# Graph attention in one launch: a group of heads leaves PSUM one slot later, and a finished graph is summed behind the attention

## The reference, cut to what matters

```
mask = adjacency + eye > 0                       # first network
for l in range(3):
    scores = si[:, :, None] + sj[:, None, :] + attn_b[l]
    scores = where(scores >= 0, scores, 0.2 * scores); masked with -inf
    h = layernorm(x + softmax(scores) @ x, g1[l], beta1[l])
    x = layernorm(h + gelu(h @ W1[l] + b1[l]) @ W2[l] + b2[l], g2[l], beta2[l])
x = layernorm(x_in + x)
xp = x @ W_proj                                  # second network, 8 heads of 32
scores[b, h, i, j] = a_src[b, h, i] + a_dst[b, h, j] + b_att[h]
out = relu(softmax(masked leaky_relu(scores)) @ xh)
result = layernorm(x + out)
```

## Time and profile before

| | us |
|---|---|
| median of 3 runs (lowest, highest) | 2346.33 (2344.75, 2347.79) |
| the profiled execution, its own time | 2346.35 |
| span of the profile, first to last instruction | 2344.6 |
| busy: PE, PE weight load | 2217.9 (95%), 1564.2 (67%) |
| busy: DVE, ACT, POOL | 1806.8 (77%), 1686.4 (72%), 184.9 (8%) |
| DMA | 29.4% of the 16 engines' span |

### The profile page before, as it was taken

One profiled execution on the slowest core, in us unless ns is written; L12 is line 12 of the kernel. 1 busy time (PEld: TensorE's weight loads), 2 busy tenths in 40 slices (PEclk: granted clock), 3 DMA queues, 4 the chain that ended last, 5 costly groups with the idle time before them and its releaser, 6 DMA issues.

```text
span 2344.6 us, 32312 instructions
## 1 busy us (share of the span) xinstructions
PE 2217.9 (95%) x10497; PEld 1564.2 (67%) x10497; DVE 1806.8 (77%) x5718; ACT 1686.4 (72%) x3247; POOL 184.9 (8%) x200
## 2 busy tenths in 40 slices
PE   3999999999999999999999999999999999999765
PEld 2676767666776777667676677667767666767543
DVE  5457687878788788887788787887888877676577
ACT  2434468777877778777787778777688777878685
POOL 0010110000100010000100001000100000010000
PEclk9999999999999999999999999999999999999977
DMA  6011024343072242442253331622434421200011
GB/s 217 10 36 54 10 95 147 96 131 118 28 220 86 73 139 78 153 120 75 99 162 95 126 121 29 216 86 72 140 94 137 133 72 53 73 23 19 28 46 37
DMA packets 116019, 219.57 MB, mean 94 GB/s; under 512 B 7784, under 2 KB 57228, under 8 KB 110476
## 3 DMA queue, kind: packets, MB, share of 16 engines
q1 hardware_dynamic: 115852, 217.50, 29.4%
HBM read 164.78 MB, written 52.69 MB: 93 GB/s over the span
## 4 chain that ended last, share of the span: by engine, by line
PE 75%; DVE 16%; ACT 5%; issue 2%; POOL 1%; DMA 1%; SPq 0%; DVEq 0%; POOLq 0%; ACTq 0%
PE ffn L1198 22%; PE av L1115 13%; PE ffn L1187 11%; PE av L1187 11%; PE pT L1098 8%; PE av L1139 4%; DVE prob L751 2%; PE av L1174 2%; DVE prob L742 2%; ACT prob L505 2%; ACT prob L499 1%; DVE stats L690 1%; DVE xs L868 1%; DVE xs L862 1%; PE trow L1077 1%
## 5 line engine op out<-in xcount | busy, mean ns | idle before, releaser
L1198 PE MATMUL ffn<-w_sb,G 128*128 128x256 f32 x3072 | 743.7, 382 | 0.0
L1198 PEld LDWEIGHTS ffn<-w_sb,G 128*128 128x128 f32 x3072 | 562.5, 191 | 90.7 <-issue 24.3
L751 DVE CUSTOM_DVE_ANT_0 prob<-trow,mask 128x512 f32<-128x512 f32 x704 | 458.1, 685 | 56.3 <-PE trow L1077 32.6
L1098 PEld LDWEIGHTS pT<-ident,prob 128*128 128x128 f32 x2144 | 273.1, 146 | 185.4 <-issue 115.5
L1098 PE MATMUL pT<-ident,prob 128*128 128x128 f32 x2144 | 337.1, 283 | 49.1 <-DVE prob L805 18.8
L505 ACT ACTIVATE prob<-prob,nm 128x512 f32<-128x512 f32 x512 | 363.0, 712 | 0.0
L499 ACT ACTIVATE prob<-prob,s 128x512 f32<-128x512 f32 x512 | 349.3, 715 | 13.7 <-DVE nm L758 13.0
L1187 PE MATMUL ffn<-hT,w_sb 128*128 128x512 f32 x768 | 355.0, 595 | 1.1 <-ACT hT L518 1.1
L1187 PE MATMUL av<-hT,w_sb 128*128 128x512 f32 x768 | 353.6, 593 | 0.0
L455 POOL TENSOR_TENSOR rstd<-veps,mhalf 128x4 f32<-128x4 f32 x127 | 160.0, 1260 | 2115.2 <-DVE veps L686 2115.2
L1115 PE MATMUL av<-xs,prob 128*128 128x257 f32 x1024 | 244.3, 380 | 11.1 <-DVE prob L812 11.1
(11 more groups left out here) (120 smaller groups left out, 2579.1 us busy)
## 6 DMA issues: line engine op xcount, KB each, us to landing
w_sb<-in_L_gnn_W SPq DMA_DIRECT2D x48, 1024.0 KB, 8.4
blocks_dram<-blocks SPq DMA_DIRECT2D x168, 256.0 KB, 4.2
prob<-blocks_dram SPq DMA_DIRECT2D x42, 1024.0 KB, 4.8
trow<-rows_dram SPq DMA_DIRECT2D x128, 256.0 KB, 3.3
adj_sb<-in_adj SPq DMA_DIRECT2D x16, 1024.0 KB, 7.4
xin<-in_x SPq DMA_DIRECT2D x16, 512.0 KB, 6.3
x0r<-in_x SPq DMA_DIRECT2D x16, 512.0 KB, 5.8
out<-o SPq DMA_DIRECT2D x15, 512.0 KB, 4.0
```

The lines of the kernel that those rows point to most:

```text
L751: return v.tensor_tensor_reduce(out=out_[:, t, :], in0=targets, in1=mask[:, t, :], scale=1.0, scalar=LEAST, op0=ALU.add, op1=ALU.max, accu ...
L1098: last = te.transpose(pT[bank][:, j * P:(j + 1) * P], src[:, t, j * P:(j + 1) * P], ident[:])
L1198: last = te.matmul(ffn[part][:, at:at + D], G[:, f, t * P:(t + 1) * P], w2_sb[:, g // 2 % STAGES, f, :], start=f == 0, stop=f == FT - 1)
```

## The change

`heads_out` for four heads is no longer called at the end of the unit in which PE made them, but in the next unit, between `times_gain` and `first_targets`. `graph_sum` of an even graph (slot 4) is called behind `attention` and `turn_blocks` rather than before them; that of an odd graph (slot 1) stays. `graph_out` and `plus_bias` change places. POOL's inverse deviation of an even finished graph follows that of the attention. No instruction is added or taken away.

```diff
@@ gpsimd
-                if ended(g) is not None:
+                if ended(g) is not None and ended(g) % 2:
                     inverse_deviation(LAST)
                 if first_ends(g) is not None and g + 1 < UNITS:
                     inverse_deviation(RESIDUAL)
                 if g + 1 < UNITS:
                     inverse_deviation(ATTENDED)
+                if ended(g) is not None and ended(g) % 2 == 0:
+                    inverse_deviation(LAST)
@@ vector
-                four = side_by_side(turned(g))[1]
+
+                four = side_by_side(turned(g - 1))[1] if g else None
...
                 times_gain(s, l)
+                if four is not None:
+                    heads_out(four)
                 if att:
                     first_targets(s2)
...
                 done = ended(g)
-                if done is not None:
+                if done is not None and done % 2:
                     graph_sum(done)
...
                 for q in turned_behind(g)[:1]:
                     turn_blocks(q)
+                if done is not None and done % 2 == 0:
+                    graph_sum(done)
+                plus_bias(s, l)
                 if done is not None:
                     graph_out()
-                plus_bias(s, l)
                 if att:
                     fed_forward(s, 0)
...
                 for q in new[2:]:
                     head_made(q)
-                if four is not None:
-                    heads_out(four)
```

## The result

The changed kernel takes 2340.24 us (median of 9 runs, 2338.00 to 2340.75) where the kernel before took 2347.08 (9 runs, 2344.75 to 2350.72): 6.8 us less, a ratio of 0.997 with a 95% interval of 0.996 to 0.998. The forecast was 12.3 us less, 2334.1, with a range up to 2338.0. The sign was right, the size nearly twice too large, and the median lies outside the range. The span of the profile fell from 2344.6 to 2338.5 us.

The account below looks back on a forecast made before the run. PE, busy 2217.9 us, was taken to bound the kernel, so only its waits for DVE could give time. Five units at 2.00 plus 2.27 make 12.3 us, and 2346.35 less that gives 2334.1, range 2328.5 to 2338.

Parts of the forecast that it names:

- Part 1: Slot 4: with `graph_sum` of even graphs behind the attention, PE's wait before the third product goes, 12.3 us in all.
- the 2.00 that were forecast: Slot 4: PE's third product starts 4.35 us behind the first instead of 6.35, a gain in each of five units.
- The gain in unit 46: Slot 4 of the last pair: DVE itself waits 0.67 us for PE and PE isn't waiting, so nothing is gained.
- Part 2: `heads_out` a slot later, 0.89 us on DVE, moved 27 times: no cost or gain in slots 5, 1, 3 and 4.
- PE's 0.84 us: Slot 4: PE's delay at L1077 for DVE's row sums moves to the first product, awaiting ACT's probabilities; gain 0.
- the 3.31 us of `graph_sum`: Slot 4: DVE time of its four kinds of instruction, from L937 to L800, moved behind the attention and held covered.
- the 7.85 us: Slot 4: DVE's idle time before L898, until PE's L1147, taken as cover for the moved work.
- The rival "nothing": Slot 4: PE loses the 2.00 us again later, behind `normalise` for instance, and 2346 stays; chance 0.04.
- The rival "less": Slots 1, 3, 5: `heads_out` uncovered, first targets late, 0.34 us in each of 20 slots, 6.8 us; 2340.9; chance 0.08.

Follow-up runs that it names:

- e1: The kernel before with only `heads_out` moved a slot later: 2347.70 us against 2346.68 for the kernel before, ratio 1.0005.
- e4: The changed kernel with `heads_out` of slot 4 put behind `first_targets`: 2335.08 us against 2346.68 for the kernel before.
- e3: The changed kernel with DVE waiting for GpSimd's shift ahead of `graph_sum`: 2334.91 us against 2346.68 for the kernel before.
- e6: The changed kernel with slot 4's `heads_out` split, reciprocal ahead of the targets, product between attention and `graph_sum`: 2332.88 us against 2347.48 for the kernel before.
- e7: The changed kernel with `graph_sum`'s first instruction cut into four of 128x256: 2336.70 us against 2347.48 for the kernel before.

## Why the prediction was wrong

**Part 1, the wait before the third product: right.** It is gone in all six units. In unit 16 the third product comes 1.88 us sooner behind the first, the fourth another 0.07 sooner, and the first 0.06 sooner in the unit: the 2.00 that were forecast. The gain in unit 46 was nothing, as said: it takes 47.05 us in both traces.

**Part 2, `heads_out`: right.** It was priced at nothing in four places, and e1 shows no price that can be told from none. That PE's 0.84 us would move to the first product and hang on ACT was right as well (e4).

**The step that failed** is the one that priced what was moved behind the attention. The prediction counted the 3.31 us of `graph_sum` against the 7.85 us in which DVE is idle, found them covered, and said that what DVE, POOL and ACT do behind the last `attended` "is counted from PE's fourth product and comes earlier with it". It asked whether DVE has time for the moved work, not whom the work disturbs while it runs. GpSimd's L460 is 0.2 us long and on the chain from the attention to the next state (L455, L460, L541, L1174). Of POOL the text said only that it is 8% busy and that an exchange in its list costs nothing; the second is true (e3), the first no argument. The lost 1.07 us a slot are 6.4 us in six slots; 12.3 less 6.4 is 5.9, against 5.7 found in the six units and 6.8 by the medians.

**The rival "nothing"** named the place, behind `normalise` in slot 4, without saying what would lose the time there, and got 0.04 for the whole of the gain. It took half of it. The new wait behind the attention is the sign that the prediction had named for it.

**The rival "less"** gave 2340.9, within 0.7 us of what was measured. That is coincidence. Its mechanism, first targets that come late in slots 1, 3 and 5, did not happen: in slot 5 they start 11.97 us into the unit, its own sign asked for more than 12.2, and the units 25, 27 and 29, of slots 1, 3 and 5, are as long as before (44.39, 45.29 and 44.39 us, to 0.01).

**The trace of before had it.** In slot 0 `plus_bias` follows the attention directly, and there GpSimd's multiplication was already held. This is POOL in unit 24 of the kernel before, and DVE:

```profile
1145.15 1.26 POOL L460 TENSOR_TENSOR shift<-nmean,rstd 128x4 f32<-128x4 f32 x1
```

```profile
1145.14 1.22 DVE L848 TENSOR_TENSOR xs<-xs,bias_row 128x1024 f32<-128x1024 f32 x1
```

PE in the same unit:

```profile
1151.97 1.04 PE L1174 MATMUL av<-ident,xs 128*128 128x128 f32 x8
```

PE comes to the transposes of the state much later there than in slot 4 and has no wait before them, so in slot 0 the hold cost PE nothing. But the same instruction at 0.20 and at 1.26 us in one trace is a question that has to be asked before anything is put beside it. The mean of a group of rows hides it: only every seventh of these multiplications is long.

## What to carry to other kernels

Cover is not only a matter of free time on the engine that does the work: look at which short instruction of another engine runs in that time, what it reads, and who hangs on it. Compare the shortest and the longest duration of a small GpSimd instruction whose size never changes; where they differ, look at what DVE had begun just before. A wait of 0.2 us on an engine with time to spare can be worth 1 us on the engine that has none, and moving an instruction of the wrong kind by one place can cost as much as a good reordering gains.

## What the runs showed of the hardware

GpSimd's 128x4 multiplication with its inputs in SBUF takes 0.20 us beside DVE's TENSOR_SCALAR of 128x256 with one tensor input (L945, before) and beside a TENSOR_TENSOR with one input in PSUM (L901, e6). It takes 1.26 us when a SCALAR_TENSOR_TENSOR (L939) or TENSOR_TENSOR (L850, L848) of 1.22 us with both inputs in SBUF has begun 0.01 us before it, and 0.46 beside the first of four pieces of the former (e7). So it is held until that one instruction has ended. That is how the Trainium skill has it ("SBUF — State Buffer", Who interferes with whom): a DVE instruction with two SBUF inputs contends with a GpSimd instruction that reads SBUF, and whichever comes first has the shared ports until it is done. That it takes a GpSimd instruction that reads SBUF is the page's word alone: in every case here GpSimd's inputs were in SBUF. By the rule an estimate from the rows of slot 0 would have been a gain of some 6 us, the 12.3 less six times 1.06 (1.26 - 0.20).

The profile shows this as a longer GpSimd instruction and not as idle time, and its list of waits names L460 as the releaser of ACT, never DVE as that of L460. In single units of nearly every trace DVE is 0.35 us late without a visible cause (unit 28 of the changed kernel takes 47.87 us against 47.53 in unit 16, and its DVE stands idle for 0.50 us before L683 with its own L692 named); what makes it was not tried.
